# First stage of a graph layer on one core: two row groups and two key banks in another order, degrees as products on TensorE, a bias addition moved beside attention

## The chip, the cores and the metric

The program runs on one core of a Trainium2 chip. The metric is device time in microseconds (us) of one execution. The kernel before takes 808.77 us (median of three runs, 807.51 to 809.99). Engines are called PE (TensorE), DVE (VectorE), ACT (ScalarE), POOL (GpSimd) and SP (SyncE, which only issues DMAs here). Each engine executes its own instructions in order; they wait for each other through semaphores.

## The reference, cut to what matters

One layer over 1250 nodes with 512 features and 40,000 edges sorted by destination:

```python
xn = layernorm(x)
agg = segment_sum(xn[src], dst);  cnt = segment_sum(1, dst)      # degree of every node
h = xn @ w_self.T + (agg / max(cnt, 1)) @ w_neigh.T + bias
gnn = relu(layernorm(h) * gamma + beta)
q, k, v = split(xn @ w_qkv)                                       # 8 heads of 64
q_phi, k_phi = elu(q @ proj) + 1, elu(k @ proj) + 1
kv = k_phi.T @ v;  z = 1 / (q_phi @ k_phi.sum(0))
mix = (q_phi @ kv * z) @ w_proj + b_proj
x = x + gnn + mix
x = x + moe_ffn(layernorm(x))                                     # shared part and 8 experts
```

## The kernel before, in words

The 1250 rows are 10 tiles of 125. Nearly every product is made of three f16 products (high x high, high x low, low x high; `split3`), so that a 125x512 result over 512 inputs is 12 matmuls. What follows is the part that the change touches, the time up to the end of attention.

**First stage.** DVE takes the statistics of x (`bn_stats`), ACT the square root, DVE scales (`norm`); rows come in three groups of 4, 4 and 2 tiles (`GROUPS`). PE turns each tile (`turn_x`, L1285, into banks 0 and 1), ACT copies it out as f16 (`xT_high`, L440), DVE writes the low half (`xT_low`, L760). Beside this the projection is multiplied into the key and query weights: four `fold`s on PE (L1291) for the keys, each taken out by `wp_high` (ACT, L446) and `wp_low` (DVE, L767), through banks 2 and 7. Then for every tile: `keys_mm` (12 matmuls, L1268, into bank 6), `key_phi` on ACT (two Relu, L454 and L455, and an Exp, L457, into a scratch of two buffers), `key_sum` on DVE (L777), `values_mm` (12 matmuls, bank 7), `value_out` on ACT (L465), and `kvacc` (L1322, four f32 products that add k_phi.T @ v up in banks 3 and 5). `rows_high` (ACT, L436) and `rows_low` (POOL, L327) make f16 copies of the normalized rows. `unit(u)` converts a block of weights: a DMA brings 1 MB into one of two staging buffers, ACT writes the high half (L425), DVE the low half (L722); U_V, unit 0, is the value weights, and `values_mm` needs it. Between these DVE works out from the edge list where each sub-block of 25 destinations begins (L808 to L853).

**Count loop.** Destinations are 10 blocks of 125, each of 5 sub-blocks. The loop runs g = 0..44 over the sub-blocks of the first 9 (`NFIX`). In round g DVE makes one-hot matrices (two small instructions L858 and L859, then L864 and L867) into a ring of 4; PE multiplies them to counts (`count`, 8 matmuls, L1298); ACT copies the counts of a block out (`counts_out`, L514) to CT; and PE multiplies two tiles of the counts of the block before with the rows (`spread`, 4 matmuls, L1305). Tables place the remaining `keys_mm`, `values_mm` and query folds between rounds (`KEY_AT`, `VAL_AT`, `FOLD_AT`). POOL adds up the counts of each block over the 10 tiles in four additions (L338 to L345), and PE turns the sum into degrees with one product of one column (`degrees`, L1310). In rounds 0 to 3 DVE also makes a table of extra work (`extras_masks`, L875 to L883, which waits for a small product behind `count` 0, and `extras_table`); then a loop over the extra items runs, here once, with its own one-column products (L1440).

**Means and attention.** DVE divides the ten blocks by their degrees (L960), PE turns them (L1448), ACT and DVE write high and low (L555, L964), while PE multiplies the queries and ACT and DVE form q_phi. Attention goes tile by tile (`att` L995 and L1002 on DVE, `att_turn`, `attT_low` L1008, `project`, `mix_add` L1014) with units 3 to 8 converted on the way. POOL adds b_proj to the ten tiles of x (L350); `mix_add` waits for it. This addition waits for `ring_free`, which DVE gives at L956, just ahead of the division L960.

The order of every engine's queue is written out by hand.

## Time and profile before

| what | us |
|---|---|
| median of three runs | 808.77 (807.51 to 809.99) |
| the profiled execution, whole | 806.47 |
| its span in the trace | 804.4 |
| PE busy | 730.5 (91%) |
| DVE busy | 434.8 (54%) |
| ACT busy | 266.8 (33%) |
| POOL busy | 221.6 (28%) |

The profile is of one execution; the 2.1 us between its time and its span lie outside what the trace shows. PE is busy 91% of the span, so the time is lost where PE waits. The page's slices show this in three places: from about 20 to 60 us, from 200 to 240 us and around 600 us. The first two are the part that is described above. The chain that ended last is PE for 74% of the span and DVE for 12%.

### The profile page before, as it was taken

How to read it: one execution, taken by the hardware profiler on the slowest of the kernel's cores; microseconds unless marked ns; L12 is line 12 of the kernel's file. 1: busy time of each engine (PE TensorE's matmuls, PEld its weight loads, DVE VectorE, ACT ScalarE, POOL GpSimd, SP SyncE). 2: the span in 40 equal slices, each digit the busy share in tenths (PEclk: the TensorE clock that was granted, in tenths of full speed). 3: DMA queues.
4: the chain of work that ended last, by engine and by line, in shares of the span. 5: the costliest groups of instructions: out<-in, count | busy, mean ns of one | idle time of the engine just before them, and what ended most of it. 6: DMA issues, size and time to landing. Idle time of an engine off the chain costs nothing.

```text
span 804.4 us, 11761 instructions
## 1 busy us (share of the span) xinstructions
PE 730.5 (91%) x4108; PEld 450.5 (56%) x4108; DVE 434.8 (54%) x815; ACT 266.8 (33%) x390; POOL 221.6 (28%) x203
## 2 busy tenths in 40 slices
PE   3659999998568998998999999999969999999998
PEld 3436677776335765565566664444845555555554
DVE  4566999999646892568732642222234544311153
ACT  3563222221228530133653322333335444422000
POOL 3320235255510000000222224444632222211362
PEclk9989999999879999999999999999969999999999
DMA  9200000200002450000122411111257776443574
GB/s 250 68 0 1 1 1 1 106 1 1 13 1 84 167 195 0 1 1 0 52 58 72 156 52 26 53 53 53 55 165 277 271 279 208 145 144 117 178 204 133
DMA packets 24367, 73.36 MB, mean 91 GB/s; under 512 B 7138, under 2 KB 7484, under 8 KB 20225
## 3 DMA queue, kind: packets, MB, share of 16 engines
q1 hardware_dynamic: 8607, 39.74, 14.7%
q0 software_dynamic: 10624, 24.99, 10.8%
q10 hardware_dynamic: 5090, 8.01, 2.7%
q8 instruction: 29, 0.48, 0.2%
q14 instruction: 17, 0.14, 0.1%
HBM read 57.38 MB, written 15.31 MB: 90 GB/s over the span
## 4 chain that ended last, share of the span: by engine, by line
PE 74%; DVE 12%; ACT 5%; issue 4%; DMA 2%; ACTq 1%; DVEq 1%; POOL 0%; POOLq 0%
PE banks L1268 57%; PE banks L1298 5%; PE banks L1305 4%; PE banks L1600 2%; DVE big L960 2%; ACT W L425 1%; DVE st L743 1%; PE banks L1322 1%; DMA big<-in_proj_mat 1%; PE banks L1291 1%; DVE W L722 1%; PE banks L1474 1%; DMA y_rows<-xT 1%; DMA stg<-in_units 1%; ACT big L593 1%
## 5 line engine op out<-in xcount | busy, mean ns | idle before, releaser
L1268 PE MATMUL banks<-W,xT 128*125 128x512 f16 (+1 forms) x1392 | 322.4, 386 | 21.4 <-ACT big L455 15.6
L1268 PEld LDWEIGHTS banks<-W,xT 128*125 128x125 f16 (+1 forms) x1392 | 167.0, 123 | 153.4 <-issue 34.1
L1268 PE MATMUL banks<-xT,W 128*128 128x500 f16 (+1 forms) x720 | 129.9, 342 | 1.8 <-DVE xn L1220 1.4
L1268 PEld LDWEIGHTS banks<-xT,W 128*128 128x128 f16 x720 | 70.4, 98 | 59.7 <-issue 3.1
L722 DVE SCALAR_TENSOR_TENSOR W<-stg,W 128x2048 f16<-128x2048 f32 x30 | 68.2, 2290 | 38.7 <-ACT W L425 38.6
L356 POOL TENSOR_TENSOR big<-xn,big 125x512 f16<-125x512 f32 x20 | 23.4, 1172 | 229.1 <-ACT big L608 229.1
L1268 PE MATMUL banks<-W,big 128*125 128x512 f16 x360 | 81.5, 380 | 0.0
L367 POOL DMA_INDIRECT xn<-h_rows,tokidx x28 | 35.4, 1265 | 125.4 <-PE banks L1600 119.7
L1238 DVE CAST xT<-banks 128x1024 f32 x23 | 28.1, 1222 | 73.4 <-PE banks L1600 73.4
L1268 PEld LDWEIGHTS banks<-W,big 128*125 128x125 f16 x360 | 48.3, 136 | 29.2 <-issue 2.3
L425 ACT ACTIVATE W<-stg 128x2048 f16<-128x2048 f32 x30 | 56.5, 1903 | 7.2 <-DMA stg<-in_units 7.2
L1220 DVE SCALAR_TENSOR_TENSOR xn<-banks,xn 128x500 f32<-128x500 f32 (+1 forms) x24 | 14.2, 590 | 69.8 <-ACT xn L668 67.8
L1305 PE MATMUL banks<-W,big 125*125 125x512 f16 x200 | 50.1, 379 | 1.3 <-ACT big L521 0.8
L689 ACT ACTIVATE xT<-banks 128x512 f32<-128x512 f32 x24 | 14.3, 596 | 70.7 <-PE banks L1268 48.2
L338 POOL TENSOR_TENSOR W<-big 125x625 f16<-125x625 f16 x9 | 14.7, 1632 | 80.7 <-ACT big L514 80.7
L380 POOL TENSOR_TENSOR big<-xn,big 128x500 f16<-128x500 f32 (+1 forms) x24 | 22.6, 942 | 48.7 <-ACT big L671 48.6
L864 DVE TENSOR_TENSOR W<-big 125x2000 f16<-125x2000 f16 x26 | 32.4, 1247 | 2.8 <-DVE big L859 2.7
L1305 PEld LDWEIGHTS banks<-W,big 125*125 125x125 f16 x200 | 25.7, 135 | 12.3 <-issue 1.8
L1090 DVE SCALAR_TENSOR_TENSOR xn<-banks,xn 125x512 f32<-125x512 f32 x20 | 13.8, 689 | 33.7 <-ACT xn L604 33.6
L1600 PE MATMUL banks<-ident,xn 128*128 128x128 f16 x384 | 27.4, 226 | 4.6 <-issue 3.2
L1600 PEld LDWEIGHTS banks<-ident,xn 128*128 (+1 forms) x384 | 24.8, 100 | 11.0 <-issue 5.4
L1268 PE MATMUL banks<-W,xn 128*125 128x512 f16 x120 | 27.8, 381 | 3.5 <-DVE xn L1008 3.5
(287 smaller groups left out, 892.2 us busy)
## 6 DMA issues: line engine op xcount, KB each, us to landing
stg<-in_units SPq DMA_DIRECT2D x30, 1024.0 KB, 5.4
y_rows<-xT ACTq DMA_DIRECT2D x29, 256.0 KB
h_rows<-big POOLq DMA_DIRECT2D x10, 500.0 KB, 3.6
out_x<-x SPq DMA_DIRECT2D x10, 224.0 KB
stg<-in_wqkT SPq DMA_DIRECT2D x2, 1024.0 KB, 11.4
x<-in_x SPq DMA_DIRECT2D x2, 896.0 KB
x<-in_x SPq DMA_DIRECT2D x1, 448.0 KB
xn<-h_rows,tokidx POOLq DMA_INDIRECT x28, 4.8
```

Source lines behind the costliest of these rows:

```text
L356: g.tensor_tensor(hrow[t % 2][:, HID + 512 * u:HID + 512 * (u + 1)], mscr[0:P, 1024 + 512 * u:1536 + 512 * u], hrow[t % 2][:, 512 * u:512 ...
L367: g.indirect_dma_start(hg[i % 2], None, h_rows, bass.IndirectOffsetOnAxis(ap=tokidx[:, i:i + 1], axis=0)).then_inc(g_in[i % 2], 16)
L380: g.tensor_tensor(hT[:, 1, j, c0:c0 + w], mscr[:, 1024 + 512 * (n % 2):1024 + 512 * (n % 2) + w], hT[:, 0, j, c0:c0 + w], ALU.subtract).th ...
L425: s.activation(W[:, u % NSLOT, 0, :], stg[:, u % NSTG, :], ACT.Copy, scale=WS).then_inc(S["w_h"], 1)
L722: v.scalar_tensor_tensor(out=W[:, u % NSLOT, 1, :], in0=stg[:, u % NSTG, :], scalar=WS, in1=W[:, u % NSLOT, 0, :], op0=ALU.mult, op1=ALU.s ...
L864: v.tensor_tensor(oht[z % RING], iotaK.unsqueeze(1).to_broadcast(wide), krel[k].rearrange("p (a b) -> p a b", b=2).unsqueeze(2).to_broadca ...
L960: v.tensor_scalar(aggacc[0:BLK, b, :], aggacc[0:BLK, b, :], cntacc[:, b:b + 1], None, ALU.mult).then_inc(S["an_rdy"], 1)
L1238: v.tensor_copy(hgT[:, bass.ds((i + 1) % 2, 1), 1].rearrange("p z j n -> p (z j) n"), turned[1]).then_inc(S["hg_l"], 1)
L1268: ins = te.matmul(dst, lhs(sl, c), rhs(sr, c), start=(first and c == 0 and k == 0), stop=(last and c == n - 1 and k == 2))
L1298: ins = te.matmul(ps[q][:, h * KEYS:(h + 1) * KEYS], ohp[z][:, a, :, b], oht[z][:, a, :, b], start=(a == 0 and b == 0), stop=(a == CH // 2 ...
L1305: ins = te.matmul(ps[4][0:BLK, :], CT[z][0:P, t, :], xs[:, s, t, :], start=(t == 0 and s == 0), stop=(t == TILES - 1 and s == 1))
L1600: ins = te.matmul(turned[s][:, j, :], rows(s * HID + j * 128), ident16[:, :], start=True, stop=True)
```

## The change

Six edits, all ahead of the end of attention.

- Rows are normalized in two groups, 4 tiles and 6 (`LATER`); the statistics of the later six are taken between other DVE work, with one square root for all six.
- All folds come earlier and have four banks (2, 7, 3, 6); the first two stand ahead of the first turned tile.
- The keys have two banks in turn up to tile 5 (`kbank`), and three buffers behind them (`KTMP`) instead of two; key tile 8 and value tile 3 now stand ahead of the count loop, in which keys 9 and values 4 to 9 remain.
- The four POOL additions for each block are gone. `spread` has one product of one column more for each tile of counts: 10 for each block, 90 in all, in place of 9.
- POOL's addition of b_proj waits for `q_rdy` at 12 (all of q_phi is formed) instead of `ring_free`.
- Waits that belong to these move with them.

```diff
-KEY_AT = {2: 8, 6: 9}
-VAL_AT = {0: 3, 4: 4, 10: 5, 16: 6, 22: 7, 28: 8, 34: 9}
+KTMP = 3
+KEY_AT = {3: 9}
+VAL_AT = {1: 4, 5: 5, 10: 6, 16: 7, 22: 8, 28: 9}
+LATER = (4, 6)
...
+        def kbank(t):
+            return ps[2] if t < 6 and t % 2 == 0 else ps[6]
...
-            for i in range(FIX):
-                z = i % 2
-                pool.wait_ge(S["ct_rdy"], 3 * i + 3)
...
-                g.tensor_tensor(degs[z], CT[z][0:P, 0:5, :].rearrange("p t d -> p (t d)"), CT[z][0:P, 5:10, :].rearrange("p t d -> p (t d)"),
-                                ALU.add).then_inc(S["deg_a"], 1)
...
             pool.wait_ge(S["ld_bp"], 16)
-            pool.wait_ge(S["ring_free"], 1)
+            pool.wait_ge(S["q_rdy"], 3 * PAIRS)
             for t in range(TILES):
...
             def key_phi(t):
-                o = 1024 * (t % 2)
+                o = 1024 * (t % KTMP)
                 act.wait_ge(S["k_mm"], t + 1)
-                if t >= 2:
-                    act.wait_ge(S["k_rdy"], t - 1)
+                if t >= KTMP:
+                    act.wait_ge(S["k_rdy"], t - KTMP + 1)
...
             for t in range(4):
                 rows_high(t)
-            sqrts(*GROUPS[1])
+            sqrts(*LATER)
             key_phi(0)
+            key_phi(1)
             xT_high(4)
             xT_high(5)
-            key_phi(1)
+            key_phi(2)
...
-            norm(0)
+            dve.wait_ge(S["ld_x0"], 16 * len(PARTS))
+            stats(x, 0, 4)
+            scale_rows(0, 4)
+            wp_low(0, ps[2])
+            dve.wait_ge(S["ld_x1"], 16 * len(PARTS))
+            v.bn_stats(st[:, 4, :], x[:, 4, :])
+            v.bn_stats(st[:, 5, :], x[:, 5, :])
+            wp_low(1, ps[7])
             xT_low(0)
             xT_low(1)
...
+            dve.wait_ge(S["ld_x2"], 16 * len(PARTS))
+            v.bn_stats(st[:, 8, :], x[:, 8, :])
+            link(v.bn_stats(st[:, 9, :], x[:, 9, :]))
+            for t in range(4, TILES):
+                ins = v.bn_aggr(mv[:, t, :], st[:, t, :])
+            link(ins)
+            scale_rows(*LATER)
+            key_sum(0)
+            key_sum(1)
             xT_low(4)
             xT_low(5)
-            key_sum(0)
+            key_sum(2)
             xT_low(6)
             xT_low(7)
-            norm(2)
-            key_sum(1)
+            key_sum(3)
             unit(U_V)
...
-            def spread(z, ts=range(TILES)):
+            def spread(z, ts=range(TILES), deg=None):
                 for t in ts:
+                    if deg is not None:
+                        one_col = te.matmul(kvb[0][0:BLK, 400 + deg:401 + deg], CT[z][0:P, t, :], ones16[0:P, 0:1], start=False,
+                                            stop=(t == TILES - 1), skip_group_check=True)
+                        if t == TILES - 1:
+                            one_col.then_inc(S["deg_mm"], 1)
                     for s in range(2):
...
                 if t == 0:
                     pe.wait_ge(S["wp_rdy"], 4)
-                else:
+                elif t >= 6:
                     pe.wait_ge(S["k_rel"], t)
+                elif t >= 2:
+                    pe.wait_ge(S["k_rel"], t - 1)
...
             values_mm(0)
+            keys_mm(6)
+            kvacc(0)
+            values_mm(1)
             pe.wait_ge(S["rng_T"], 1)
...
             values_mm(2)
+            keys_mm(8)
+            kvacc(2)
             pe.wait_ge(S["pool_const"], 6)
```

The order on PE from the start of the program, before. L1285 is the turning of tiles, L1291 the folds (a row of x4 is one fold), L1268 keys and values (x12 is one tile):

```order
L1285 MATMUL banks<-ident,xn 128x125 x8
L1291 MATMUL banks<-big,stg 128x128 x4
L1285 MATMUL banks<-ident,xn 128x125 x4
L1291 MATMUL banks<-big,stg 128x128 x4
L1285 MATMUL banks<-ident,xn 128x125 x4
L1291 MATMUL banks<-big,stg 128x128 x8
L1268 MATMUL banks<-W,xT 125x512 x24
L1285 MATMUL banks<-ident,xn 128x125 x8
L1268 MATMUL banks<-W,xT 125x512 x12
L1285 MATMUL banks<-ident,xn 128x125 x8
L1268 MATMUL banks<-W,xT 125x512 x24
```

The same place in the changed kernel, whose lines are L1286 for the folds, L1280 for the turning and L1263 for keys and values:

```order
L1286 MATMUL banks<-big,stg 128x128 x8
L1280 MATMUL banks<-ident,xn 128x125 x8
L1286 MATMUL banks<-big,stg 128x128 x4
L1280 MATMUL banks<-ident,xn 128x125 x4
L1286 MATMUL banks<-big,stg 128x128 x4
L1280 MATMUL banks<-ident,xn 128x125 x4
L1263 MATMUL banks<-W,xT 125x512 x36
L1280 MATMUL banks<-ident,xn 128x125 x8
L1263 MATMUL banks<-W,xT 125x512 x12
L1280 MATMUL banks<-ident,xn 128x125 x8
L1263 MATMUL banks<-W,xT 125x512 x12
```

Two folds moved ahead of the first two tiles, and three tiles of keys instead of two stand ahead of the turning of tiles 4 and 5. On PE in the count loop, blocks 1 and 2, before (L1298 counts, L1305 spread, L1310 the degrees):

```order
L1298 MATMUL banks<-W 128x250 x8
L1305 MATMUL banks<-W,big 125x512 x4
L1298 MATMUL banks<-W 128x250 x8
L1305 MATMUL banks<-W,big 125x512 x4
L1310 MATMUL banks<-ones,W 125x1
L1298 MATMUL banks<-gcat 128x250 x8
```

and in the changed kernel (L1293 counts, L1305 spread, L1300 the products of one column):

```order
L1293 MATMUL banks<-W 128x250 x16
L1300 MATMUL banks<-ones,big 125x1
L1305 MATMUL banks<-W,big 125x512 x2
L1300 MATMUL banks<-ones,big 125x1
L1305 MATMUL banks<-W,big 125x512 x2
L1263 MATMUL banks<-W,xT 125x512 x12
```

Every pair of spread matmuls has a product of one column ahead of it, and the product L1310 behind a block is gone.

## Rows read from the trace of the kernel before

**Rows 1.** Busy by stretch: start:end, length, PE, PEld, DVE, ACT, POOL busy, clock, DMA.
```profile
97.00:191.80 94.80, 94.80 (x634) 70.74 (x631) 91.53 (x166) 23.80 (x43) 44.98 (x32) 1.00 0.06 24
212.00:232.00 20.00, 7.45 (x32) 4.13 (x32) 14.96 (x13) 3.92 (x8) 12.82 (x10) 0.66 0.00 1
```
**Rows 2.** PE in order of time: start, length, instructions [idle before, releaser].
```profile
14.85 2.04 PE L1291 MATMUL banks<-big,stg 128*128 128x128 f32 x8 [0.17 <-DMA big<-in_proj_mat]
...
23.27 2.77 PE L1268 MATMUL banks<-W,xT 128*125 128x512 f16 x12 [1.50 <-DVE W L767]
28.87 4.46 PE L1268 MATMUL banks<-W,xT 128*125 128x512 f16 x12 [2.83 <-ACT big L455]
33.17 1.02 PE L1285 MATMUL banks<-ident,xn 125*128 125x125 f32 x8
...
78.97 1.07 PE L1298 MATMUL banks<-W 125*128 125x250 f16 x8
...
96.96 1.02 PE L1305 MATMUL banks<-W,big 125*125 125x512 f16 x4
```
**Rows 3.** The chain that ended last, in the count loop: start, length, what.
```profile
98.88 0.90 PE banks L1298 x8
99.78 0.86 PE banks L1305 x4
100.64 2.59 PE banks L1268 x12
...
114.74 0.89 PE banks L1322 x8
```
**Rows 4.** ACT in the first stage, in order of time.
```profile
28.75 1.28 ACT L457 ACT_TABLE_LOAD   x1
...
63.95 0.60 ACT L454 ACTIVATE big<-banks 125x512 f32<-125x512 f32 x1 [4.55 <-DVE xn L777]
...
65.44 0.60 ACT L465 ACTIVATE xn<-banks 125x512 f32<-125x512 f32 x1
```
**Rows 5.** DVE in the first stage and the first rounds, in order of time.
```profile
28.59 1.91 DVE L755 TENSOR_SCALAR xn<-x,mv,rs 125x512 f32<-125x512 f32 x4
...
47.98 2.29 DVE L722 SCALAR_TENSOR_TENSOR W<-stg,W 128x2048 f16<-128x2048 f32 x1 [2.32 <-ACT W L425]
...
56.60 0.66 DVE L808 TENSOR_REDUCE big<-big 80x4 f32<-80x500 int32 x1
...
62.90 0.36 DVE L829 TENSOR_REDUCE big<-big 80x50 f32<-80x200 f32 x1
...
80.20 0.15 DVE L875 COPY big<-banks 10x1 f32<-10x1 f32 x1 [0.25 <-PE banks L1396]
...
83.47 0.41 DVE L883 TENSOR_SCALAR big<-big 10x390 f32<-10x390 f32 x1
```
**Rows 6.** Products of one column on PE: shortest/median/longest ns, first and last start.
```profile
L1310 PE MATMUL banks<-ones,W x9: 166/167/167, 108.4 to 197.1; 125*125 125x1 f16 x9
L1440 PE MATMUL banks<-ones,big x10: 167/196/197, 208.7 to 209.2; 125*125 125x1 f16 x10
```
**Rows 7.** PE at the end of the count loop, in order of time.
```profile
199.06 1.08 PE L1298 MATMUL banks<-W 125*128 125x250 f16 x8 [1.84 <-DVE W L867]
```
**Rows 8.** The division, POOL's addition and the row scaling: shortest/median/longest ns.
```profile
L960 DVE TENSOR_SCALAR big<-big,etabs x10: 1306/1482/1491, 211.2 to 223.6; 125x512 f32<-125x512 f32 x10
L350 POOL TENSOR_TENSOR x<-x,bproj x10: 1264/1441/1455, 210.9 to 223.4; 125x512 f32<-125x512 f32 x10
L755 DVE TENSOR_SCALAR xn<-x,mv,rs x10: 540/542/547, 12.1 to 44.5; 125x512 f32<-125x512 f32 x10
```
**Rows 9.** PE behind the division, in order of time.
```profile
225.84 1.06 PE L1448 MATMUL banks<-ident,big 125*128 125x125 f32 x4 [11.27 <-DVE big L964]
226.70 4.54 PE L1268 MATMUL banks<-xT,W 128*128 128x500 f16 x12
```
**Rows 10.** POOL's first addition beside a weight block's L722 on DVE.
```profile
48.55 2.74 POOL L327 TENSOR_TENSOR W<-xn,W 125x512 f16<-125x512 f32 x1 [9.33 <-ACT W L436]
```

More of the change, by code:

```diff
@@ L508, in _ @@
             value_out(1)
+            key_phi(7)
             value_out(2)
-            key_phi(7)
+            key_phi(8)
+            value_out(3)
             def counts_out(i, q):
@@ L799, in _ @@
             xT_low(9)
-            key_sum(2)
+            key_sum(4)
             dve.wait_ge(S["xs_l"], 7)
@@ L1306, in spread @@
                 return ins
-            def degrees(i):
-                pe.wait_ge(S["deg_rdy"], i + 1)
-                te.matmul(kvb[0][0:BLK, 400 + i:401 + i], degt[i % 2], ones16[0:P, 0:1], start=False, stop=True, skip_group_check=True).then_inc(S["deg_mm"], 1)
             def xl(t):
@@ L1346, in _ @@
             fold(0, ps[2])
+            fold(1, ps[7])
+            turn_x(0)
+            turn_x(1)
+            fold(2, ps[3])
             turn_x(2)
-            fold(1, ps[7])
+            fold(3, ps[6])
             turn_x(3)
-            pe.wait_ge(S["wp_rdy"], 1)
-            fold(2, ps[2])
-            pe.wait_ge(S["wp_rdy"], 2)
-            fold(3, ps[7])
             keys_mm(0)
             keys_mm(1)
+            keys_mm(2)
             turn_x(4)
             turn_x(5)
-            keys_mm(2)
+            keys_mm(3)
             turn_x(6)
             turn_x(7)
-            keys_mm(3)
             keys_mm(4)
@@ L1382, in _ @@
             te.matmul(ps[4][0:NBLK, 0:1], scr[0:1, 2610:2610 + NBLK], one[0:1, 0:1], start=True, stop=True).then_inc(S["ex_col"], 1)
-            keys_mm(7)
-            kvacc(2)
+            values_mm(3)
+            kvacc(3)
             pe.wait_ge(S["xT_rdy"], TILES)
@@ L1407, in _ @@
                             pe.wait_ge(S["agg_ev"], i - 1)
-                    part = spread((i - 1) % 2, range(2 * j, 2 * j + 2))
+                    part = spread((i - 1) % 2, range(2 * j, 2 * j + 2), i - 1)
                     if j == SUBS - 1:
                         part.then_inc(S["agg_mm"], 1)
-                        degrees(i - 1)
                 if g in KEY_AT:
@@ L1425, in _ @@
             pe.wait_ge(S["agg_ev"], FIX - 1)
-            spread((FIX - 1) % 2).then_inc(S["agg_mm"], 1)
-            degrees(FIX - 1)
+            spread((FIX - 1) % 2, deg=FIX - 1).then_inc(S["agg_mm"], 1)
             pe.wait_ge(S["tab_rdy"], 1)
```

81 lines of the change are left out of this document (27 added, 54 removed).

## The prediction, made before the changed kernel was run

> **What bounds the kernel now.** I read the stretches first, then the chain in order of time, then PE's own rows with what released each wait. Three regimes stand in the part that changes. Up to the first count (78.97 us, rows 2) PE waits: for the weights that DVE finishes (1.50 us ahead of the first keys), then for ACT to empty the only key bank (2.83 us), and the tile behind that wait runs at 4.46 us instead of 2.77 [rows 2]. From 97 to 191.8 us PE is busy all 94.8 us and DVE 91.5 [rows 1]: the count loop is PE's, DVE is close behind, and the chain is made of PE pieces [rows 3]. At 212 to 232 us PE is busy 7.5 of 20 us with a mean clock of 0.66 [rows 1], because it waits 11.27 us [rows 9] for the ten divisions L960, each 1482 ns at the median, while POOL's additions L350 run in the same interval at 1441 ns; the same operation in the same shape, L755, takes 542 ns with POOL idle [rows 8].
>
> **1. The stage ahead of the first count.** What PE must do there after the change: 9 tiles of keys and 4 of values, each 2.59 us, and 4 kvacc of 0.89 [rows 3], so 33.7 + 3.6 = 37.3 us, and the turning of six tiles, 2.7 us (two tiles take 1.02 with the tail of the last [rows 2]). With 0.5 us for small products it is 40.5 us. Before, the same stretch from 23.27 to 78.97 us held 8 keys, 3 values and 3 kvacc, 28.5 + 2.7, with the turns and small ones 34.4 us of work in 55.7: 21.3 us were waits or the slow clock.
>
> I place the waits that remain by going through the queues. The folds start at 14.85 us, when the projection's DMA has landed [rows 2]; now the first turned tiles stand behind two of them, and a bank is free for each fold. The eight small groups end about 23 us. On DVE the fourth weight half now comes behind two pairs of statistics, one of which lies under PE's own work, so the first keys start about 24.3 us, 1 us later than before. Keys 1 follow at once in the second bank. Keys 2 wait until ACT has emptied bank 2, and ACT stands at the square root of the second group until DVE has the statistics of rows 8 and 9: about 29.1 us; relus to 30.1, so keys 2 start at 30.1 (0.6 us lost). The exponential needs a table load of 1.28 us [rows 4]; with one later group in place of two there is no second one. An ACT pass over a tile takes 65.44 - 63.95 = 1.49 us [rows 4], so keys 3, 4 and 5 start about 33.6, 37.1 and 40.6. DVE scales six rows, 6 x 0.48 = 2.9 us (1.91 for four, rows 5), to 32.8. Values 0 wait for the value weights: ACT reaches them at 41.0, 1.8 there and 2.2 on DVE [rows 5], so 45.1, 1.9 us lost. Then keys 6 47.7, values 1 51.2, keys 7 54.2, values 2 58.0, keys 8 60.6, values 3 64.2, kvacc 3 to 68.3. DVE's chain over the edge list took 56.60 to 63.26 [rows 5]; it starts about 47.0 and is through at 53.0, ahead of the place where PE asks. The first count would start at 68.3 against 78.97: 10.7 us earlier, with 3.5 us of waits in 44. The bounds: with none of these waits 14 us; if keys with their ACT pass stay in step as before, so that half the old 21.3 us remains, 4 us.
>
> **2. The count loop.** Rounds 0 to 5 change shape. The table of extra items waits for the product behind count 0, then takes DVE from 80.20 to 83.88 [rows 5], 3.7 us. Before, values 3 stood over it; now only count 1 does, and PE waits 3.0 us. With values 4, keys 9, three counts and kvacc 4 behind it I get count 5 through at 84.6; before it was 96.96 [rows 2], so 12.4 us ahead. From there to 191.8 PE has the same rounds less one tile of keys and one kvacc, 2.59 + 0.89 = 3.5 us, and less eight old products. It has 80 new products of one column. Their price is the one number here that decides anything. L1440 issued ten of them, each with new weights, 208.7 to 209.2 [rows 6], 0.056 us apart. Each new one has its weights loaded under a long matmul and leaves the next load uncovered, so I take 0.054 us: 4.3 us. The low end is what the old L1310 cost: at 108.4 it pushed the next count by about 0.03, 2.4 us in all. The high end is its full 0.167 us [rows 6], 13.4 us. So from 97 on the loop is 4.3 - 3.5 - 0.3 = 0.5 us longer, and with part 1 the loop's end is 11.9 us earlier.
>
> The trace prices the load at 0.056 us by L1440 [rows 6]. The Trainium skill, TensorE: Matmul & The Clock Gate, section LDWEIGHTS, gives a weight load as its columns over 1.2 in ns, 104 ns for 125 columns, which speaks against this edit: by it the 80 would cost 8.3 us and the time would be 4 us above my figure; it lies inside the range.
>
> POOL's 36 additions go from beside this loop. PE has no wait there that they cause, so I price that at nothing until the end; PE was busy throughout [rows 1], and a plain round becomes 0.90 + 0.86 [rows 3] + 0.11 = 1.87 us. The cover is gone only at the end, where DVE is the later one: PE waits 1.84 us for one-hots [rows 7], and DVE had been held by POOL. Without that four extra counts follow each other and the group ends 1.6 us earlier, after ten more products (0.5 us).
>
> **3. The division.** L960 took 211.16 to 225.1. At L755's pace, 0.48 us apart, ten take 4.8 us instead of 13.95: 9.1 us. Nothing else stands over it: the turned blocks that PE wants wait for L964, which is behind all ten on DVE's queue. The query tile behind the gap ran at 4.54 us [rows 9] at the lower of the two clock levels, against about 2.6 when PE had worked; with 2 to 3 us of idle in place of 11 it may run at either, 0 to 1.9 us. I take 1.2, in all 10.3 (9.1 to 11.0). What is late next is L964 behind the tenth division, already counted.
>
> **4. Attention.** POOL's ten additions now start with the last q_phi and take 12 to 14 us. `mix_add` asks for one behind each projection, and a projection alone is 2.59 us of PE [rows 3] against 1.44 of POOL [rows 8], so it should wait for none. They do run beside DVE: POOL took 2.74 us for an addition that began 0.6 us into L722 [rows 10], so the two exclude each other. The Trainium skill (SBUF — State Buffer, section SBUF: two separate sides) says that DVE is shut out only where it has two SBUF inputs or a two-port mode; by that rule only the L722s of attention wait, not its operations on PSUM. Two or three L722 fall into the additions, each waiting for at most one of 1.2 to 1.4 us, and the weight chain sets the pace of these tiles: 1 us lost (0 to 4).
>
> **The sum.** 11.9 + 1.6 + 10.3 - 1.0 = 22.8 us off the profiled 806.5 (span 804.4 and 2.1 around it): 783.7. The profiled execution lies 2.3 us under the median of the runs, so the median becomes 786.0.
>
> **Rivals.**
> - The first stage gives back much less: the normalization of six rows, which ACT and DVE now wait for in one piece, moves the keys behind it, and DVE's table in round 1 stands alone. For it: PE's waits there end with DVE or ACT [rows 2], and both keep all their work. Against it: the second bank lets a tile run through. With 4 us instead of 10.7 the time is 792.7.
> - Each product of one column costs its full 0.167 us (nothing overlaps): 90 x 0.113 more, 10.2 us: 796.2. For it: its recorded length; against it: L1440 issued faster.
> - The division stays slow because it has a cause of its own: 10.3 less, 796.3. Against it: L755 in rows 8.
> - Slower than before: every product of one column adds into the same column as the one before it in its block, and if PE must let each finish behind the long matmul before it, it costs a whole matmul's 0.38 us. Without its products the change gains 27.6 us; 90 at 0.38 are 34.2, so 6.6 us slower, 815.4. It decides from 0.307 us each. Against it: nothing in the trace shows a drain, since kvacc and spread add up in one bank at full pace.
>
> **How the numbers follow.** Forecast 0.74; less in the first stage 0.12; full price of the product 0.06; slow division 0.03; drained products 0.03; the rest 0.02. The forecast's own spread is 781 to 790. The range 779.5 to 794 reaches into the first rival and leaves out some 2 in 10. Runs of one kernel agree within 0.3% (2.4 us), so that is what can be told from no change. Faster 0.96, same 0.01, slower 0.03.
>
> **What would show it.** The first count near 68 us and count 5 through near 85; a PE wait near 3 us in round 1; in the loop a new product every 0.054 us more, so a plain round of 1.87 us; the ten divisions at 542 ns and under 5 us in all; the query tile behind them below 4.5 us; POOL's additions from the last q_phi on, and one or two L722 of attention starting over 1 us after ACT's half. I am wrong if the first count is after 74 us, if a plain round is above 2.0 us, or if L722 in attention waits at every tile.

## The result, and the profile after

The changed kernel takes 794.23 us (median of four runs, 793.57 to 795.91), the kernel before 808.73 us beside it; the ratio is 0.982 (0.980 to 0.985). A second set of five runs gave 793.48 us, ratio 0.982 (0.980 to 0.985). It is faster by 14.5 to 15.1 us (1.8%, clear of the noise) where 22.8 were forecast. Its 794.23 us lie 0.2 us above the range of 779.5 to 794, those of the second set 0.5 below its upper end. The profiled execution took 793.57 us, its span is 791.5, and PE is busy 93% of it.

All that follows is read from where the same work starts. The columns are the start before, the shift that the prediction's terms add up to, and the shift in two profiles of the changed kernel, the second from the set of five (span 790.2), all in us.

| work on PE | before | forecast | first profile | second profile |
|---|---|---|---|---|
| first count | 78.97 | -10.7 | -11.5 | -11.1 |
| first spread | 96.96 | -12.4 | -11.2 | -9.3 |
| last block's spread | 192.71 | -11.9 | -10.1 | -8.2 |
| spread of the extra item | 204.32 | -13.5 | -8.0 | -7.6 |
| attention | 257.96 | -23.8 | -20.1 | -19.8 |
| first tile behind attention | 306.81 | -22.8 | -17.1 | -17.0 |
| expert loop | 589.92 | -22.8 | -17.0 | -17.0 |
| shared output | 744.09 | -22.8 | -12.9 | -14.3 |

**Up to the first spread**, PE in order of time (start, length, instructions, in brackets the idle time before and what ended it). These rows answer to [rows 2].

```profile
14.20 3.75 PE L1286 MATMUL banks<-big,stg 128*128 128x128 f32 x16 [14.20 <-DMA big<-in_proj_mat]
...
23.55 5.36 PE L1263 MATMUL banks<-W,xT 128*125 128x512 f16 x24 [1.33 <-DVE W L749]
29.40 2.77 PE L1263 MATMUL banks<-W,xT 128*125 128x512 f16 x12 [0.49 <-ACT big L440]
...
43.90 4.31 PE L1263 MATMUL banks<-W,xT 128*125 128x512 f16 x19 [1.39 <-DVE W L707]
...
67.49 1.08 PE L1293 MATMUL banks<-W 125*128 125x250 f16 x8
...
72.47 0.81 PE L1397 MATMUL banks<-big,ones 10*1 10x390 f32 x2 [2.77 <-DVE big L878]
...
74.09 4.22 PE L1263 MATMUL banks<-W,xT 128*125 128x512 f16 x12
...
85.76 0.62 PE L1305 MATMUL banks<-W,big 125*125 125x512 f16 x2
```

The order of the waits is the forecast one: 0.49 us ahead of keys 2 (0.6 forecast), 1.39 ahead of values 0 (1.9), and no tile at the old 4.46 us; a wait of 0.78 us for ACT ahead of kvacc 3 was not forecast. Then comes the wait for DVE's table of extra items, 2.77 us where 3.0 were forecast. What was not forecast stands behind it: the value tile at 74.09 takes 4.22 us, and 5.38 in the second profile, where 2.8 is full pace. From 74.1 to 76.0 us PE's granted clock is 0.50, the lower of its two levels.

**The count loop and its end**, by stretch as in [rows 1], then PE in order of time:

```profile
86.00:181.60 95.60, 95.60 (x683) 72.08 (x681) 81.01 (x166) 22.23 (x40) 0.00 (x0) 1.00 0.06 23
203.00:221.00 18.00, 12.75 (x79) 7.85 (x78) 9.26 (x19) 7.32 (x14) 0.00 (x0) 1.00 0.00 1
```

```profile
183.08 0.17 PE L1300 MATMUL banks<-ones,big 125*125 125x1 f16 x1
183.11 0.62 PE L1305 MATMUL banks<-W,big 125*125 125x512 f16 x2
183.57 0.17 PE L1300 MATMUL banks<-ones,big 125*125 125x1 f16 x1
...
189.52 1.78 PE L1293 MATMUL banks<-W 125*128 125x250 f16 x8 [1.87 <-issue]
191.10 1.87 PE L1293 MATMUL banks<-gcat 125*128 125x250 f16 x8
...
196.34 4.53 PE L1305 MATMUL banks<-W,big 125*125 125x512 f16 x20 [0.55 <-ACT big L532]
...
207.96 0.62 PE L1444 MATMUL banks<-ident,big 125*128 125x125 f32 x4 [3.16 <-DVE big L959]
208.42 2.70 PE L1263 MATMUL banks<-xT,W 128*128 128x500 f16 x12
```

PE is still busy in all of the loop, and DVE has fallen from 91.5 of 94.8 us [rows 1] to 81.0 of 95.6: POOL, which no longer works there, had been holding it (with POOL's additions back it is 91.9 of 96.0, below). A pair of long products with its product of one column in front comes every 0.49 us, against 0.43 in a spread of [rows 3] (0.86 for two pairs): 0.056 us for the small one.

At the end of the loop PE's wait is as long as it was (1.84 us in [rows 7], 1.87 now), and it was not for one-hots before either, although [rows 7] names DVE. The first extra count needs only the first of the extra one-hots (the wait on `x_oh`). In the kernel before, in order of time, DVE, PE and ACT:

```profile
188.72 1.28 DVE L864 TENSOR_TENSOR W<-big 125x2000 f16<-125x2000 f16 x1
189.93 0.88 DVE L867 TENSOR_TENSOR W<-big 125x1024 f16<-125x1024 f16 x1
```

```profile
197.05 0.17 PE L1310 MATMUL banks<-ones,W 125*125 125x1 f16 x1
```

```profile
197.25 0.60 ACT L521 ACTIVATE big<-banks 125x512 f32<-125x512 f32 x1 [4.68 <-PE banks L1305]
```

DVE had that one-hot at 190.81 us, 8 us ahead of the count at 199.06; L867 of a later one ended at 198.64, and the wait is probably put down to that. PE's last product ended at 197.22, ACT's copy of the block at 197.85, and the count came 1.2 us behind the copy. In the changed kernel the copy ends at 188.28, and the count comes 1.2 us behind it, too. That 1.2 us is the reading of the number of items into PE's register (shown below by moving it). The wait is 1.84 to 1.93 us in all eleven profiles that leave this place as it was, with POOL's additions and without. The counts behind it are not at full pace in this profile: 1.78 and 1.87 us in place of 1.08; in the second profile they are.

**Division, addition and weights**: the instructions of one line (shortest, median and longest ns, first and last start), as in [rows 8], then DVE's weight blocks in attention and PE's last projection in order of time.

```profile
L955 DVE TENSOR_SCALAR big<-big,etabs x10: 481/482/487, 203.2 to 206.7; 125x512 f32<-125x512 f32 x10
```

```profile
L335 POOL TENSOR_TENSOR x<-x,bproj x10: 1265/1273/3318, 241.5 to 256.6; 125x512 f32<-125x512 f32 x10
```

```profile
247.69 3.34 DVE L707 SCALAR_TENSOR_TENSOR W<-stg,W 128x2048 f16<-128x2048 f32 x1 [1.12 <-ACT W L410]
253.01 2.52 DVE L707 SCALAR_TENSOR_TENSOR W<-stg,W 128x2048 f16<-128x2048 f32 x1
258.05 2.29 DVE L707 SCALAR_TENSOR_TENSOR W<-stg,W 128x2048 f16<-128x2048 f32 x1 [0.45 <-ACT W L410]
```

```profile
285.36 4.39 PE L1263 MATMUL banks<-W,xn 128*125 128x512 f16 x12 [3.50 <-DVE xn L1003]
```

The same projection in the kernel before:

```profile
304.08 2.80 PE L1268 MATMUL banks<-W,xn 128*125 128x512 f16 x12 [3.51 <-DVE xn L1008]
```

The ten divisions fell from 1482 ns [rows 8] to 482, PE's wait behind them from 11.27 us to 3.16, and the query tile from 4.54 [rows 9] to 2.70. POOL's additions now cost two weight blocks 1.05 and 0.23 us over the 2.29 of a free one. The last projection stands behind a wait of 3.50 us and takes 4.39; before it had the same wait and took 2.80.

**The expert loop**: what PE waited for (total us, times, longest), before and after, each between 565 and 745 us.

```profile
PE banks L1268 <- ACT xT L689: 2.2, 4, 1.4
```

```profile
PE banks L1263 <- ACT xT L674: 6.6, 5, 1.7
```

The line is ACT's copy of an expert's result into the one buffer from which it is stored (`yb`), and the copy waits until the store before has landed; no edit touches it, and the loop took 158.3 us against 154.2.

### The profile page after: what moved, and what is told of

Read it like the earlier page. It is cut to its first block, busy times and chain, and to the rows that moved or that the text cites. A ratio compares the mean times of both kernels' runs of the same rounds, so it can differ in the third digit from the quotient of the medians.

```text
span 791.5 us, 11867 instructions
## 1 busy us (share of the span) xinstructions
PE 732.8 (93%) x4189; PEld 454.4 (57%) x4189; DVE 410.8 (52%) x809; ACT 263.3 (33%) x387; POOL 171.9 (22%) x167
## 3 DMA queue, kind: packets, MB, share of 16 engines
q0 software_dynamic: 10624, 24.99, 11.1%
## 4 chain that ended last, share of the span: by engine, by line
PE 73%; DVE 9%; ACT 7%; DMA 6%; issue 3%; POOL 1%; ACTq 1%; DVEq 0%; POOLq 0%
PE banks L1263 53%; PE banks L1305 6%; PE banks L1293 6%; DMA y_rows<-xT 3%; ACT W L410 2%; PE banks L1596 2%; PE banks L1318 1%; PE banks L1286 1%; DMA big<-in_proj_mat 1%; DVE W L707 1%; DVE st L728 1%; ACT xT L674 1%; DMA stg<-in_units 1%; PE banks L1470 1%; DMA xn<-h_rows,tokidx 1%
## 5 line engine op out<-in xcount | busy, mean ns | idle before, releaser
L1263 PE MATMUL banks<-W,xT 128*125 128x512 f16 (+1 forms) x1392 | 319.4, 384 | 11.7 <-ACT xT L674 6.6
L1263 PEld LDWEIGHTS banks<-W,xT 128*125 128x125 f16 (+1 forms) x1392 | 166.1, 122 | 142.3 <-issue 22.4
L1263 PE MATMUL banks<-xT,W 128*128 128x500 f16 (+1 forms) x720 | 128.1, 339 | 1.8 <-DVE xn L1215 1.4
L1263 PEld LDWEIGHTS banks<-xT,W 128*128 128x128 f16 x720 | 69.8, 97 | 58.3 <-DVE xn L1215 1.7
L707 DVE SCALAR_TENSOR_TENSOR W<-stg,W 128x2048 f16<-128x2048 f32 x30 | 69.4, 2333 | 41.5 <-ACT W L410 41.5
L1263 PE MATMUL banks<-W,big 128*125 128x512 f16 x360 | 81.5, 380 | 0.0
L1263 PEld LDWEIGHTS banks<-W,big 128*125 128x125 f16 x360 | 48.3, 136 | 29.2 <-issue 2.3
L335 POOL TENSOR_TENSOR x<-x,bproj 125x512 f32<-125x512 f32 x10 | 16.4, 1680 | 194.2 <-DVE big L970 194.2
L1305 PE MATMUL banks<-W,big 125*125 125x512 f16 x200 | 54.1, 393 | 0.6 <-ACT big L532 0.6
L674 ACT ACTIVATE xT<-banks 128x512 f32<-128x512 f32 x24 | 14.3, 597 | 75.0 <-PE banks L1263 50.8
L1263 PE MATMUL banks<-W,xn 128*125 128x512 f16 x120 | 29.5, 398 | 3.5 <-DVE xn L1003 3.5
L395 POOL DMA_INDIRECT xT<-y_rows,sloti x20 | 25.9, 1296 | 20.3 <-DMA y_rows<-xT 8.7
```

Source lines behind the costliest of these rows:

```text
L395: g.indirect_dma_start(yg[n % 4], None, y_rows, bass.IndirectOffsetOnAxis(ap=sloti[:, 0, k, t:t + 1], axis=0)).then_inc(yg_in[n % 4], 16)
L707: v.scalar_tensor_tensor(out=W[:, u % NSLOT, 1, :], in0=stg[:, u % NSTG, :], scalar=WS, in1=W[:, u % NSLOT, 0, :], op0=ALU.mult, op1=ALU.s ...
L1263: ins = te.matmul(dst, lhs(sl, c), rhs(sr, c), start=(first and c == 0 and k == 0), stop=(last and c == n - 1 and k == 2))
L1305: ins = te.matmul(ps[4][0:BLK, :], CT[z][0:P, t, :], xs[:, s, t, :], start=(t == 0 and s == 0), stop=(t == TILES - 1 and s == 1))
```

## The experiments

Each run's expectation was written before it ran. Medians are of 4 to 10 runs, ratios are to the kernel before on the same chip.

**One part at a time: the bias alone.** The kernel before, with POOL's additions moved:

```diff
-            pool.wait_ge(S["ring_free"], 1)
+            pool.wait_ge(S["q_rdy"], 3 * PAIRS)
```

> The kernel before with one edit of the six: the bias addition waits for the last q_phi. Theory A (the edits add up as the two traces show them): the ten divisions take about 4 us in place of 14 and the query tile behind them runs at full clock, 12 us gained; attention gives back 1.4 us through two locked weight conversions; the median is about 10 to 11 us under before, 798. Theory B (the lock moves with the additions and costs the same beside attention): within 3 us of before. A third reading, that the expert loop far behind loses time whenever the front end moves, gives 802, with PE waits for ACT in the expert loop above 4 us as in the changed kernel.

Measured: 800.21 us, 0.991 (0.988 to 0.994). The ten divisions take 477 ns each, so POOL's additions alone had made them slow, and the rival in which they have a cause of their own falls. So does the third reading: PE's waits for ACT in the expert loop are 2.9 us. From the extra spread to attention it is 44.8 us against 53.6 before. In the changed kernel it is 41.5; here both query tiles behind DVE waits ran slowly (4.38 and 3.93 us where 2.70 is full pace), 3.3 us in all, more than the 2.2 that the time lies above the 798 of theory A.

**The degrees back on POOL**, everything else as changed:

```diff
-    part = spread((i - 1) % 2, range(2 * j, 2 * j + 2), i - 1)
+    part = spread((i - 1) % 2, range(2 * j, 2 * j + 2))
     if j == SUBS - 1:
         part.then_inc(S["agg_mm"], 1)
+        degrees(i - 1)
```

and with them POOL's loop of four additions for each block, as before.

> The changed kernel with the degrees formed as before: four additions on POOL and one product for each block. Theory A (the 90 products of one column cost about 0.056 us each on PE and buy nothing): the loop from count 5 to the last spread is 4 to 5 us shorter, the end of the extra counts is given back by DVE's one-hots being late, in all 3 us faster than the changed kernel, 791. Theory B (POOL's port use beside the loop costs DVE what the products cost PE): the same time within 1 us, 794.

Measured: 788.64 us, 0.976 (0.971 to 0.980), 4.8 us under the changed kernel. The products of one column cost more than POOL's additions cost anyone. The trace gives 3.5 us of it, from the first spread to the end of the last block's (98.4 us for 101.9 in the second profile). POOL's additions are not free: they hold DVE, and PE waits twice for one-hots late in the loop, 0.90 and 0.35 us. The wait ahead of the extra counts is again put down to DVE:

```profile
180.83 1.74 DVE L882 TENSOR_TENSOR W<-big 125x1024 f16<-125x1024 f16 x1
```

```profile
188.13 1.08 PE L1313 MATMUL banks<-W 125*128 125x250 f16 x8 [1.93 <-DVE big L882]
```

But the one-hot that this count needs was finished at 182.57 us, so it is the same wait for ACT's copy and the register as in the kernel before, and not DVE's.

**The first stage left as it was**, degrees and bias changed:

> The changed kernel without the new order of the first stage: the kernel before with the products of one column and the moved bias. Theory A: the first stage is worth 11.5 us at count 5, and its two tiles more ahead of the loop 3.5 us less of loop; so this is 13 to 15 us slower than the changed kernel, 808, hardly faster than before. Theory B (the first stage's gain is mostly lost in round 1, where PE now waits alone for the table): 7 us slower than the changed kernel, 801.

Measured: 808.10 us, 0.999 (0.996 to 1.001). So the first stage is worth 14.6 us (808.10 - 793.48; 13.3 by the two ratios, since the kernels before beside them differ by 1.2 us). Without it the other two parts nearly cancel: the bias gives 7 by the run above, the products take 5. The count loop, 100.3 us from its first spread to its last before, is 105.3 here: 5.1 us for 90 products.

What went from the first stage is shown by the page of the kernel before, in the row of keys and values (busy us, mean ns, then PE's idle time ahead of them and what ended most of it):

```profile
L1268 PE MATMUL banks<-W,xT 128*125 128x512 f16 (+1 forms) x1392 | 322.4, 386 | 21.4 <-ACT big L455 15.6
```

These 15.6 us are six waits for ACT to empty the one key bank, of which 0.49 us is left; the tiles behind two of them (at 28.87 and 44.36) took 4.46 and 5.32 us. The two row groups, the earlier folds and the second key bank were not tried one by one, so their shares are not shown.

**A second product of one column in front of each**, into a column that nothing reads:

```diff
+    te.matmul(kvb[0][0:BLK, 440 + deg:441 + deg], CT[z][0:P, t, :], ones16[0:P, 0:1],
+              start=False, stop=(t == TILES - 1), skip_group_check=True)
```

> The changed kernel with every product of one column issued twice (the second into columns that nothing reads): 90 more. Theory A, that each costs one uncovered weight load of 0.054 to 0.060 us: 5 us slower than the changed kernel, 799. Theory B, that a product alone costs its recorded 0.167 us: 15 us slower, 809. Theory C, that the load hides beneath the long matmul ahead of it and the product is nearly free (0.03): under 3 us, 797 or less.

Measured: 797.34 us, 0.985 (0.981 to 0.989), 3.9 us over the changed kernel. The loop grew by another 5.1 us (101.9 to 107.0), 0.057 us each; a full price of 0.167 would be 15 and a drained product 34. The time alone would hardly tell theory A (799) from theory C (797 or less); the loop does.

**The changed kernel again**, as the measure for the runs beside it:

> The changed kernel as it is, as the reference of the three runs beside it. Every theory: 794 us (793 to 796), a ratio to before of 0.982. What it tells apart is inside its profile: if the 4.1 us that the expert loop lost in the first profile (158.3 us from the loop's first product to the shared output's, 154.2 before) belong to the change, they stand here too (157.5 or more); if they come and go from one execution to the next, the stretch is 153 to 156.5 us here and the profiled execution is that much shorter.

Measured: 793.48 us. The expert loop takes 156.9 us here, between the two forecasts. The first spread is 1.9 us later than in the first profile, most of it in the tile behind the table (5.38 us for 4.22).

**The last keys in round 0**, so that PE has work beside DVE's table:

```diff
-KEY_AT = {3: 9}
+KEY_AT = {0: 9}
```

> The changed kernel with one number of the table of rounds changed: the last key tile is computed in round 0 in place of round 3, so 2.6 us of PE lie beside DVE's table of extra items. Theory, that the table alone cost the 2.77 us of wait and, by the slow clock behind it, the 1.47 us of the value tile: PE waits under 0.6 us in round 1, the value tile takes 2.75 us, the first spread starts at 81.5 to 82.5 us in place of 85.8, and the time is 790 us (789 to 791.5). Rival, that DVE is then the later one through the next rounds, since it has the same operations from the table on and runs close behind PE: the wait goes from round 1 but one-hots are waited for in rounds 2 to 6, the first spread is earlier by under 2 us, and the time is 792.5 or more.

Measured: 790.58 us, 0.978 (0.976 to 0.981). Half for each: the time is that of the theory and the value tile runs at full pace, but DVE's 3.7 us come back as two waits for one-hots, 3.0 us in all, as the rival says. The first spread starts at 85.22 us, not at 82.

```profile
74.17 2.80 PE L1263 MATMUL banks<-W,xT 128*125 128x512 f16 x12
...
81.39 1.08 PE L1293 MATMUL banks<-W 125*128 125x250 f16 x8 [1.59 <-DVE W L862]
83.85 1.50 PE L1293 MATMUL banks<-W 125*128 125x250 f16 x8 [1.39 <-DVE W L862]
85.15 0.20 PE L1300 MATMUL banks<-ones,big 125*125 125x1 f16 x1
```

**The number of items read earlier**, and ACT's copy waited for ahead of the extra spread:

```diff
+    pe.wait_ge(S["tab_rdy"], 1)
+    items = pe.value_load(tab[0:1, 2 * ITEMS:2 * ITEMS + 1], min_val=1, max_val=ITEMS)
     spread((FIX - 1) % 2, deg=FIX - 1).then_inc(S["agg_mm"], 1)
-    pe.wait_ge(S["tab_rdy"], 1)
-    pe.wait_ge(S["agg_ev"], FIX)
-    items = pe.value_load(tab[0:1, 2 * ITEMS:2 * ITEMS + 1], min_val=1, max_val=ITEMS)
...
+                pe.wait_ge(S["agg_ev"], FIX)
                 spread(0)
```

> The changed kernel with two things at the loop's end in another place on PE: the number of extra items is read into a register ahead of the last spread in place of behind it, and the wait for ACT's copy of the last block stands ahead of the extra spread in place of ahead of the extra counts. Theory, that those two made the gap ahead of the extra counts once DVE was no longer late (0.60 us for ACT, 1.23 us of issue) and that the gap dropped the clock: the gap goes to under 0.3 us, the four extra counts take 4.7 to 5.0 us in place of 6.28, the extra spread starts 3 us earlier against the last spread's end (6.0 to 6.6 us behind it in place of 8.7), and the time is 791 us (790 to 792.5). Rival, that the register's read costs its 1.2 us wherever it stands, since PE's sequencer stops for it: the extra spread is earlier by 0.6 to 1.2 us only and the time is 793 or more.

Measured: 789.87 us, 0.978 (0.975 to 0.981), an interval that overlaps the unedited one's. The time is the theory's, the trace the rival's: it gives 1.3 us (extra spread 196.68 to 195.36), and the gap ahead of the counts is gone and stands with the reading where the reading went (1.59 us, where ACT alone had made it 0.78). The rest of the 3.6 us is not accounted for.

```profile
185.05 0.21 PE L1300 MATMUL banks<-ones,big 125*125 125x1 f16 x1 [1.59 <-issue]
...
189.99 1.07 PE L1293 MATMUL banks<-W 125*128 125x250 f16 x8
```

**The bias beside the query stage** in place of attention:

```diff
-            pool.wait_ge(S["q_rdy"], 3 * PAIRS)
+            pool.wait_ge(S["an_rdy"], NBLK)
```

> The changed kernel with POOL's ten additions waiting for the tenth division in place of the last q_phi, so that they run beside the query stage (about 207 to 222 us) and not beside attention. Theory, that DVE's operations on two inputs in SBUF are what POOL shuts out: attention gives back the 1.4 us that its L707s had waited (3.34 and 2.52 us in place of 2.29), but the query stage's sums on DVE with two SBUF inputs (L970, 606 ns each, eleven) take up to 1.4 us each while the additions last; eight or nine of them fall there, PE is ahead of DVE by the four query banks and waits at the end of the stage for what DVE is late, 1 to 4 us; in all 793 to 797 us. Rival, that POOL's additions cost DVE nothing in the query stage because DVE waits there for ACT's exponentials anyway (2.4 us in all): L970 keeps its 606 ns or is hidden, and the time is 792.5 (791.5 to 793).

Measured: 793.54 us, 0.982 (0.978 to 0.985), no change. The weight blocks of attention are back at 2.29 us and attention is 1.3 us shorter than in the second profile (50.4 for 51.6 us), but it starts 1.3 us later against the extra spread, where a query tile was slow again (3.63 us). The question of the two theories was not put: POOL's additions ran from 208.8 to 221.2 us, and the first of the sums L970 starts at 225.67. What DVE does beside them is L959, with one source in PSUM, and it takes 675 ns as without them (674).

**Products in the two waits.** Eleven in round 1, fourteen ahead of the last projection, into banks that are overwritten before they are read:

```diff
+    for _ in range(11):
+        te.matmul(ps[2][0:P, :], xT[:, 0, 0, 0:P], Wqp[:, 0, 1, 0, :], start=True, stop=True)
     pe.wait_ge(S["ex_sum"], 1)
...
+    if t == TILES - 1:
+        for _ in range(14):
+            te.matmul(ps[0][0:P, :], attT(t - 1)[:, 0, 0, :], unitv(U_PROJ)(0, 0), start=True, stop=True)
     pe.wait_ge(S["tT_rdy"], t + 1)
```

> The changed kernel with products that nothing reads put into two of PE's waits: eleven in round 1 (2.4 us of the 2.77 that it waits for DVE's table) and fourteen ahead of the last projection of attention (3 us of 3.5). They add nothing to the results and take no time that PE did not wait. Theory, that the tiles behind these waits run at the lower clock level because PE idled: the value tile behind the first takes 2.75 to 3.0 us (4.22 and 5.38 in the two profiles of the changed kernel), the projection behind the second 2.8 (4.39 and 4.38), and the time is 790 us (789 to 791.5). Rival, that the clock is dropped there by something else than PE's idling (both waits stand behind f32 turns or small products), so that the same tiles stay above 4 us: 793.5 us or more, and the products only cost.

Measured: 785.30 us, 0.971 (0.969 to 0.974): 8.2 us under the changed kernel by products that compute nothing. PE in order of time, at both places:

```profile
69.85 2.54 PE L1397 MATMUL banks<-W,xT 128*125 128x512 f16 x11
72.78 0.81 PE L1399 MATMUL banks<-big,ones 10*1 10x390 f32 x2 [0.39 <-DVE big L878]
...
74.18 2.80 PE L1263 MATMUL banks<-W,xT 128*125 128x512 f16 x12
...
84.43 0.62 PE L1305 MATMUL banks<-W,big 125*125 125x512 f16 x2
...
280.36 3.19 PE L1488 MATMUL banks<-W,xn 128*125 128x512 f16 x14
284.02 2.80 PE L1263 MATMUL banks<-W,xn 128*125 128x512 f16 x12 [0.48 <-DVE xn L1003]
```

The table is ready at the same time, so nothing that PE waits for came sooner; only the clock is different. It is 1.00 in the value tile (74.2 to 76.9 us) and in the last projection, where the second profile has 0.50 in the value tile (74.7 to 79.8). The first spread starts at 84.43, 3.2 us ahead of the second profile, and the last projection is back at 2.80 (1.6 us). Between the two profiles, 6.9 us apart, these 4.8 us are not all: 1.5 us were lost again in the extra counts, which ran slowly behind their wait as in the first profile (a clock of 0.59), and the expert loop took 153.1 us, 3.8 less than in the second profile, which no edit explains (below). So the two filled waits are worth 4.8 us, and the rest of the 8.2 may come and go.

**The result's copy ahead of the store's wait**, with two buffers (`yz` is that of `i % 2`) and one store in flight as before:

```diff
-    act.wait_ge(S["y_st"], 16 * i + 16)
-    s.activation(yb, ps[4][:, :], ACT.Copy).then_inc(S["y_cp"], 1)
+    s.activation(yz, ps[4][:, :], ACT.Copy).then_inc(S["y_cp"], 1)
+    high(i + 1)
+    act.wait_ge(S["y_st"], 16 * i + 16)
```

> The changed kernel with two buffers for the expert loop's result on ACT: PE's bank is copied out at once and the wait for the store before stands ahead of the next store, no longer ahead of the copy; one store is in flight as before. Theory, that the 3.4 to 6.6 us that PE waited for this copy (L674) were the stores' landing time, which comes out short or long by the store: PE's waits for the copy fall under 1 us in all, the expert loop takes 151.5 to 153 us (158.3 and 156.9 in the two profiles), and the time is 790 us (788.5 to 791). Rival, that the next wait takes over (the stores queue behind each other, ACT is late with the turned rows instead): the loop stays above 155 us and the time above 792.

Measured: 790.72 us, 0.977 (0.975 to 0.980); 2.8 us gained, with overlapping intervals. PE's waits for the copy fall from 5.1 to 2.7 us (under 1 was expected), the loop only from 156.9 to 155.3, which the rival said, though not the time.

**All edits together, with the degrees on POOL:**

> The changed kernel with the degrees back on POOL, the last keys in round 0, the number of items read ahead of ACT's waits before the last spread and ACT's copy waited for behind the extra counts, the copy of the expert results ahead of the store's wait, and fourteen products in the wait ahead of the last projection. By adding up what each gave alone or should give: 793.5 - 4.9 (degrees) - 2.9 (keys) - 2 to 3.6 (items) - 3 to 4 (store) - 1.5 (projection) = 777 to 779 us. Rival, that they overlap: PE freed in the count loop waits for DVE, whose one-hots were 91.5 us of 94.8 before and which POOL's additions hold again at the loop's end, so that of the first three only one and a half count: 782 us or more.

Measured: 787.38 us, 0.972 (0.970 to 0.975). The rival holds. What PE waited for between 66 and 212 us:

```profile
PE banks L1316 <- DVE W L885: 5.4, 4, 2.5
```

DVE is held by POOL (busy 94.9 of the 100 us from 90 to 190, 79.9 in the run with two filled waits), so PE's head start is handed back one wait at a time.

**The same with the degrees on PE**, the last keys in round 3 and both waits filled, the number of items read ahead of ACT's waits too:

> The changed kernel with its products of one column kept, the eleven and fourteen products in PE's two waits, the number of items read ahead of ACT's waits before the last spread with ACT's copy waited for behind the extra counts, and the copy of the expert results ahead of the store's wait. Theory, that these four stand in different places and so add up, unlike those of the run before, in which POOL's additions on the degrees had DVE late: 785.3 - 1.3 to 3.6 (items) - 2.8 (store) = 779 to 781 us, with no PE wait for one-hots over 0.5 us in the count loop. Rival, that a gain ahead of the expert loop is taken back there by the landing times of the stores: 784 us or more.

Measured: 785.33 us, 0.971 (0.968 to 0.973): no gain over the two filled waits. The time is the rival's, its cause is not: the gain was gone ahead of the expert loop. The extra spread is 2.9 us earlier than there (192.05 for 194.97) and attention 0.4 us later; in between, both query tiles behind a DVE wait ran slowly.

```profile
203.65 0.62 PE L1448 MATMUL banks<-ident,big 125*128 125x125 f32 x4 [3.15 <-DVE big L962]
204.10 4.38 PE L1266 MATMUL banks<-xT,W 128*128 128x500 f16 x12
...
211.43 0.98 PE L1448 MATMUL banks<-ident,big 125*128 125x125 f32 x4 [2.09 <-DVE big L962]
212.20 4.06 PE L1266 MATMUL banks<-xT,W 128*128 128x500 f16 x12
```

**Those two waits filled as well**, thirteen and eight products:

```diff
     pe.wait_ge(S["an_rdy"], b + 1)
+    for _ in range({2: 13, 5: 8}.get(b, 0)):
+        te.matmul(qb[b // 3 + 1][:, 0:500], Wqp[:, 0, 0, 0, 0:128], xT[:, 0, 0, 0:500], start=True, stop=True)
```

> The kernel of the run before with products that nothing reads also in the two waits of the query stage (thirteen in the one of 3.2 us, eight in the one of 2.1 us). Theory, that the lower clock needs PE idle right ahead of the tile: the query tiles run at 2.70 us (4.38 and 4.06 before), attention starts 3 us earlier against the extra spread (41.8 us behind it in place of 44.8), and the time is 782 us (781 to 783.5). Rival, that the clock is owed to something longer than the wait ahead of it and comes down at the next tile behind any other wait: the query tiles are fast and a stretch behind them that was at full clock is not, and the time stays at 785 us.

Measured: 782.58 us, 0.968 (0.965 to 0.971), the fastest kernel of the study: 10.9 us under the changed one. Attention starts 41.4 us behind the extra spread in place of 44.8, and no stretch behind it slowed down in exchange up to the expert loop (4.6 us ahead there). The expert loop itself took 157.2 us for 154.6 in the profile before, again without an edit. The median is 2.8 us under that of the run before.

```profile
199.63 2.91 PE L1446 MATMUL banks<-xT,W 128*128 128x500 f16 x13
202.87 0.65 PE L1450 MATMUL banks<-ident,big 125*128 125x125 f32 x4 [0.33 <-DVE big L962]
203.35 2.70 PE L1266 MATMUL banks<-xT,W 128*128 128x500 f16 x12
...
209.38 2.70 PE L1266 MATMUL banks<-xT,W 128*128 128x500 f16 x12
```

## Why the prediction was right in kind and 8 us too fast

The differences of the table's columns give the sum by the prediction's own terms (second profile against forecast): first spread 3.1 us short, loop 0.6, its end 2.2, division 1.9 more than forecast, attention 1.8 short, expert loop 2.7 short; 8.5 in all. The 1.9 us that the division gave beyond its forecast hide that the other terms miss by 10.4.

- **First stage: right to the first count** (-11.1 and -11.5 for -10.7), each tile within 1.2 us of its place. That the stage is worth the most is shown by the run without it (14.6 us). Its rival, less in the first stage, is out.
- **Round 1: the failed step.** "PE waits 3.0 us. With values 4, keys 9, three counts and kvacc 4 behind it I get count 5 through at 84.6." The wait was sized well; the tile behind it was priced as if PE had not idled. I had used the slow query tile behind the 11 us wait [rows 9] as a term of its own, and the slow key tile behind 2.83 us in [rows 2], and did not apply either to the wait that I was adding. From the first count to the first spread the forecast has 16.3 us (68.3 to 84.6), the two profiles 18.3 and 19.8, and with the wait filled it is 16.6: the step that failed is the clock behind this wait, 2.0 to 3.5 us.
- **The products of one column: right.** 0.054 us each were forecast, 0.056 to 0.057 measured, in the pitch of the loop and by doubling them. Full price and drained products are out. The Trainium skill (TensorE: Matmul & The Clock Gate, section LDWEIGHTS) prices a weight load by its columns, 104 ns for 125; taken whole as the price of such a product it is out too, since the trace has 0.056 us here. What the term lacked was the other side of the account. PE is what bounds the loop, and all that POOL's additions cost it were 1.3 us of waits for one-hots: 5.1 us for the new products less 0.3 for the old ones and these 1.3 are the 3.5 that the loop lost (4.8 by the medians). The prediction named this price and put it in a sum with gains of other parts, which hid that this part alone is a loss.
- **The loop's end: failed, by a wrong reading of a wait.** "Without that four extra counts follow each other and the group ends 1.6 us earlier". The wait of [rows 7] was taken for one-hots because the row names DVE's L867. The one-hot that PE needed there had been ready for 8 us; the wait was for ACT's copy (0.6) and the reading of PE's register (1.2), which no edit touches. It stayed at 1.87 us, and the ten more products came on top: 0.6 us later where 1.6 earlier was forecast (2.1 later in the first profile, with the slow counts).
- **Division: right, and more.** 482 ns for 542, 4.0 us for all ten where 4.8 were taken, and the query tile at full pace in the profile (1.84 us gained for 1.2). The tile's share is luck: behind the same wait it ran slowly in eight of thirteen profiles. The bias run shows that POOL's additions were the whole cause.
- **Attention: mechanism right, size off.** Two weight blocks were held, 1.3 us in all for 1.0. The other 1.6 us are again the clock, behind a wait that was there before, too. In ten of the eleven profiles of kernels that leave this wait unfilled, the kernel before in two variants among them, the projection takes 4.3 to 5.4 us; the one exception is the profile that the prediction was read from (2.80). A single profile had shown a stretch that mostly isn't so.
- **Expert loop: not forecast, and its cause stays open.** It takes 153.1 to 158.3 us over eleven profiles with the store as it was, and goes roughly with PE's waits for the copy (2.2 us at 153.1 and at 154.2, 3.9 at 156.1, 5.5 at 156.3, 5.1 at 156.9, 6.6 at 158.3). The copy waits for the landing of the store before. The changed kernel's first-stage order is in the shortest and in the longest. That the stores' landing varies is shown: in the first profile two that ACT waited for landed about 5.5 and 7.0 us behind their issue. Why it does, and whether an earlier arrival at the loop matters, is not. With two buffers the waits are 1.4 to 3.4 us, but the loop took 154.6 to 157.2 us over four profiles, so no shorter loop is shown.

## What to carry to other kernels

When an edit leaves PE waiting 2 to 4 us, price the tile behind the wait at both clock levels, also where the profile at hand shows the fast one; products that compute nothing, placed in the wait, are a cheap test and here the largest gain found (4.8 us at the first two places in the traces, 8.2 in the medians). Price each part of a change against the engine that bounds its stretch: work moved from an idle engine to the bounding one has to pay by what it frees, and 90 small products of 5.1 us freed 1.3. Before you count on a wait to go, look when the engine that the row names had finished what this very instruction needs, and list everything else that must be there, PE's own register reads included.

## What the runs showed of the hardware

- PE's clock behind a wait. Behind the 2.77 us in round 1 the tile took 4.22 to 5.38 us for 2.8 in all seven profiles that left it unfilled; the granted clock in it was 0.50 in both profiles of the changed kernel (from 74.1 to 76.0 and from 74.7 to 79.8 us), 1.00 with the wait filled. Behind the 3.16 us ahead of the second query tile it ran at full pace in five profiles and slowly in eight: 2.70 us in both of the changed kernel and 3.81 in the run with two store buffers, which is alike up to there. The extra counts behind their 1.87 us were slow in four profiles of the eleven. Waits of equal length differ, so the length alone does not decide; with the wait filled all but 0.3 to 0.5 us, the tile was at full pace each time, nine of nine in the four runs that filled one or more.
- Reading a value into PE's register behind ACT's copy left PE idle for 1.2 to 1.3 us in eleven profiles. Moved to stand behind other waits, it made a gap of 0.78 us one of 1.59. Ahead of waits that PE has anyway it was hidden (no gap of its own in the last three runs).
- POOL and DVE: a POOL addition beside DVE's ten divisions makes each wait for the other (1482 and 1441 ns in turns, [rows 8]); alone they take 482 and 1265. A weight block on DVE (2.29 us) can hold a POOL addition for most of its length: the longest of POOL's took 3.32 us. DVE's L959, with a source in PSUM, kept its pace beside POOL (675 ns, 674 without).
